# Value products and attention outputs in turn on TensorE, in a windowed-attention and convolution kernel

## The reference

```python
x = x + _L0_conv_ref(_gn(x), W_qkv, W_out, rel_height, rel_width)
x = x + _L1_conv_ref(_gn(x), weight, bias)

# inside _L0_conv_ref: windows of 8x8 queries, 12x12 keys, 4 heads of 32 channels
attn = jnp.einsum('bnd,bmd->bnm', q, k)
attn = attn + rel_pos_emb(q, rel_height, rel_width) + FIXED_MASK
attn = jax.nn.softmax(attn, axis=-1)
out = jnp.einsum('bnm,bmd->bnd', attn, v)
...
return jnp.einsum('bchw,oc->bohw', out, W_out)
```

## Time and profile before

| | |
|---|---|
| time, median of 3 runs | 3672.58 us (3671.35 to 3673.6) |
| profiled execution, its own time | 3670.79 us |
| span of its trace | 3669.0 us |
| PE busy | 3487.6 us (95%) |
| DVE busy | 3365.2 us (92%) |
| ACT busy | 2975.3 us (81%) |
| POOL busy | 2576.8 us (70%) |
| mean granted TensorE clock | 0.991 of full |

### The profile page before, as it was taken

The page is one execution under the profiler, slowest core; times in us unless marked ns, Lnnn a source line. Parts: engine busy times, 40 slices in busy tenths (PEclk is TensorE's granted clock), DMA queues, the critical chain, the costliest instruction groups (busy, mean ns, idle before and its releaser), DMA issues. The chain is left out here.

```text
span 3669.0 us, 127399 instructions
## 1 busy us (share of the span) xinstructions
PE 3487.6 (95%) x51720; PEld 2485.3 (68%) x51720; DVE 3365.2 (92%) x5646; ACT 2975.3 (81%) x5323; POOL 2576.8 (70%) x3345
## 2 busy tenths in 40 slices
PE   0699999999999999899999999999699999999999
PEld 0588888888888878688888888888544444444444
DVE  9799999999999999899999999999799888888887
ACT  0789999999999989799999999999587777777774
POOL 1577777777777777677777777777476666666664
PEclk9999999999999999999999999999899999999999
DMA  9443444344434433233333333333334433443342
GB/s 377 126 128 115 131 132 125 115 131 132 123 116 132 127 83 104 76 90 104 104 98 90 104 104 98 90 104 95 111 144 155 155 146 152 155 153 144 154 155 84
DMA packets 497157, 464.06 MB, mean 126 GB/s; under 512 B 10176, under 2 KB 469824, under 8 KB 478144
## 3 DMA queue, kind: packets, MB, share of 16 engines
q1 hardware_dynamic: 496576, 455.92, 38.9%
HBM read 321.40 MB, written 134.48 MB: 124 GB/s over the span
## 5 line engine op out<-in xcount | busy, mean ns | idle before, releaser
L1001 POOL TENSOR_TENSOR sb_tf<-sb_cf 128x1024 f32<-128x1024 f32 x256 | 609.3, 2381 | 378.6 <-DVE sb_tl L980 370.4
L513 PE MATMUL ps_t<-sb_ident,sb_d 128*108 128x128 f32 x4096 | 664.1, 285 | 5.6 <-ACT sb_pt L706 4.2
L533 PEld LDWEIGHTS ps_s<-sb_kf,sb_qb 128*64 128x64 f32 x16384 | 519.9, 138 | 180.7 <-issue 167.4
L655 DVE TENSOR_TENSOR sb_qb<-ps_q,sb_own_head 128x1024 f32<-128x1024 f32 x512 | 621.2, 1213 | 14.1 <-PE ps_q L495 14.1
L789 POOL TENSOR_TENSOR sb_erel<-sb_brel 128x288 f32<-128x288 f32 x512 | 351.6, 687 | 380.8 <-DVE sb_brel L601 373.0
L897 PE MATMUL ps_c<-sb_th,sb_wc_h 128*128 128x512 f16 x1536 | 584.8, 381 | 20.9 <-DVE sb_tl L980 20.8
L533 PE MATMUL ps_s<-sb_kf,sb_qb 128*64 128x54 f32 x16384 | 586.4, 225 | 11.6 <-DVE sb_scores L635 11.6
L897 PE MATMUL ps_c<-sb_th,sb_wc_l 128*128 128x512 f16 x1536 | 583.7, 380 | 0.0
L897 PE MATMUL ps_c<-sb_tl,sb_wc_h 128*128 128x512 f16 x1536 | 583.6, 380 | 0.0
L819 POOL TENSOR_TENSOR sb_zl<-sb_zf,sb_zh 128x396 f16<-128x396 f32 x512 | 480.9, 939 | 82.5 <-ACT sb_zh L772 82.4
L805 POOL TENSOR_TENSOR sb_prod<-sb_rel,sb_shift 128x192 f32<-128x192 f32 x1024 | 502.7, 512 | 0.0
(11 more groups left out here) (124 smaller groups left out, 8298.0 us busy)
## 6 DMA issues: line engine op xcount, KB each, us to landing
sb_xb<-rows SPq DMA_DIRECT2D x128, 780.0 KB, 7.3
sb_xc<-x SPq DMA_DIRECT2D x64, 1280.0 KB, 5.4
sb_x<-rows SPq DMA_DIRECT2D x128, 512.0 KB, 4.1
x<-sb_x SPq DMA_DIRECT2D x128, 512.0 KB, 3.7
out<-sb_oc SPq DMA_DIRECT2D x64, 1024.0 KB, 3.9
sb_abuf<-rows SPq DMA_DIRECT2D x16, 2048.0 KB, 12.0
sb_st<-rows SPq DMA_DIRECT2D x64, 512.0 KB, 5.1
sb_raw<-wconv SPq DMA_DIRECT2D x1, 576.0 KB, 3.6
```

The source lines that it names most:

```text
L513: last = pe.transpose(ps_t[0:KV, wj * 128:(wj + 1) * 128], d[:, at:at + KV], ident[:])
L533: last = pe.matmul(s_at, qb[:, qc:qc + QB], kf[:, kc:kc + KR], start=True, stop=True)
L655: dve.tensor_tensor(view(qb, 0, 128, vh * QBW + p * NW * QB, [[QB, NW], [QN, HEADS], [1, QN]]), view(ps_q, 0, 128, 0, [[QN, NW], [0, HEADS ...
L1001: pool.tensor_tensor(tf[:, k * TF:(k + 1) * TF], view(cf, 0, 128, c0 + ra * W, [[2 * W, PAIRROWS], [1, W]]), view(cf, 0, 128, c0 + rb * W, ...
```

## The change

The two loops over the parities, first all twelve value products and then all sixteen outputs, become one loop. In it each value product is followed at once by one or two outputs: the first product of a parity by heads 0 and 1, the second by head 2, the third by head 3. The semaphore waits of both stand ahead of the loop, the two signals behind it. The same 28 matmuls are issued with the same operands; no DMA and no instruction of another engine is touched.

```diff
-                            for p in range(PAR):
-                                for c, (z, w) in enumerate(PRODUCTS):
-                                    last = pe.matmul(ps_v[0:KV, p * C:(p + 1) * C],
...
-                            last.then_inc(sem["v_mm"], 1)
...
-                            for p in range(PAR):
-                                py, px = divmod(p, 2)
-                                for hd in range(HEADS):
...
+                        for p in range(PAR):
+                            py, px = divmod(p, 2)
+                            for c, (z, w) in enumerate(PRODUCTS):
+                                if own:
+                                    last_v = pe.matmul(ps_v[0:KV, p * C:(p + 1) * C],
+                                                       z_at(z, vslot, p, GW * WK * vg, [[1, KV]]),
+                                                       w[:, 2 * C:3 * C], start=(c == 0), stop=(c == 2))
+                                for hd in ((0, 1), (2,), (3,))[c] if outputs else ():
...
+                                    last_o = pe.matmul(o_at, v_at, p_at, start=True, stop=True)
+                        if own:
+                            last_v.then_inc(sem["v_mm"], 1)
+                        if outputs:
+                            last_o.then_inc(sem["o_mm"], 1)
```

More of the change, by code:

```diff
@@ L539, in body @@
                             project(n, (g + 1) % PAR, slot + ahead, u + ahead, MOMENTS.get(u) if g == 1 else None)
-                        if on(n - 3, GT):
-                            m = n - 3
+                        own, outputs = on(n - 3, GT), on(n - 4, GT)
+                        if own:
                             vslot, vg = (slot, 0) if g == 3 else (slot - 1, g + 1)
-                            need(pe, sem["vf_done"], m)
-                            for p in range(PAR):
-                                for c, (z, w) in enumerate(PRODUCTS):
-                                    last = pe.matmul(ps_v[0:KV, p * C:(p + 1) * C],
-                                                     z_at(z, vslot, p, GW * WK * vg, [[1, KV]]),
-                                                     w[:, 2 * C:3 * C], start=(c == 0), stop=(c == 2))
-                            last.then_inc(sem["v_mm"], 1)
-                        if on(n - 4, GT):
+                            need(pe, sem["vf_done"], n - 3)
+                        if outputs:
                             m, par = n - 4, g % 2
@@ L563, in body @@
                                                 [[128, GW], [1, QN]])
-                                    last = pe.matmul(o_at, v_at, p_at, start=True, stop=True)
-                            last.then_inc(sem["o_mm"], 1)
+                                    last_o = pe.matmul(o_at, v_at, p_at, start=True, stop=True)
+                        if own:
+                            last_v.then_inc(sem["v_mm"], 1)
+                        if outputs:
+                            last_o.then_inc(sem["o_mm"], 1)
                         if on(n - 3, GT):
```

## The result

The changed kernel takes 6198.8 us (median of 4 runs, 6191.8 to 6201.6) against 3672.1 us for the kernel before: a ratio of 1.688 (95% interval 1.686 to 1.690). The forecast was 6450 us with a range of 5180 to 6980. The drains and the swinging clock both came; the clock's part was smaller than forecast.

What follows compares the result with a forecast made beforehand. TensorE was taken to bound the attention phase. Drains and open weight loads add 3.80 us a turn and the low clock 1.65; 511 turns of 5.45 us on 3671 give 6456 us, forecast as about 6450, range 5180 to 6980.

Steps and rivals of the forecast that it cites:

- TensorE sets the pace, and 511 turns multiply: Attention phase: TensorE binds, so time added to its block counts once in each of 511 turns of 4.83 us.
- The drain, 0.15 us each way: Between value products and outputs: each change of weight width takes about 0.15 us, against 0.055 for a same-width successor.
- The open load of 108 columns, 0.05 us: Before outputs following a value product: their weight load is no longer hidden and adds 0.05 us.
- the second half of a float32 matmul, 0.08: Within each head's outputs: the second record starts 0.08 us after the first, not 0.055.
- The lower bound: Block of value products and outputs: open loads might be hidden, making it 4.3 us and the whole run 5180 us.
- The clock: Thin new block makes the granted clock fall and swing: 1.65 us more a turn, about 6450 us; chance 0.46.
- A fall in the block is undone in the dense rest of the turn, so about 4 us low in every turn: Each attention turn: the clock falls in the block and recovers during dense work, about 4 us low.
- The sign that was named, a mean granted clock near 0.85: Changed profile: a turn of about 10.3 us with mean granted clock near 0.85 would show a swinging clock.
- The clock holds: Rival for the new block: width changes drain but the clock stays full, 5613 us (5180 to 5725); chance 0.38.
- No drain: Rival: alternating neighbours drain cheaply or not at all, but heads no longer share the array, about 4000 us; chance 0.08.
- faster: Rival: outputs run in the shadow of value products and width changes vanish, 3640 us; chance 0.03.
- What is moved for the others: Shifted signals and waits for ACT's copies stay hidden and cost nothing; without that cover 0.3 us a turn, 150 us.

Runs made afterwards that it cites:

- 5180: Not a run: the lower end, in us, of the forecast range of 5180 to 6980 for the changed kernel, which measured 6198.8 us.
- the wide-output pair: Every output matmul takes all 128 value columns as weights, in the changed kernel's alternating order and in the earlier grouped order: 5130.2 and 5119.2 us.
- 7 excursions: Changed kernel with parities 0 and 1 alternating, 2 and 3 grouped: 4674.3 us; for 10, only parity 3 grouped: 5535.7 us.
- the last kernel: Kernel before with its grouped outputs moved directly ahead of the scores, ACT's copy of ps_o behind that of the second transposes: 3656.8 us, ratio 0.9961.

## Why the prediction was right

Step by step, by its own terms:

- **TensorE sets the pace, and 511 turns multiply.** Right. In every kernel here the time follows the turn of TensorE, and the busy time of DVE, ACT and POOL differs from before by no more than 60 us in any of them. The turns are even: from 500 to 900 us their mean is 4.83 us before, as the one turn read.
- **The drain, 0.15 us each way.** Right, also for the way back that the trace of before did not show (0.15 us from the last output to the next product). That it goes with the width and not with data type, tile or waits was argued there from one row; the wide-output pair shows it.
- **The open load of 108 columns, 0.05 us, and the second half of a float32 matmul, 0.08.** 0.04 and 0.08. The block came to 5.03 us for 5.15, and the drains' part to 1880 us for 1942. The lower bound (loads pulled ahead across the change, 4.3 us) is excluded.
- **The clock.** The direction was right and the term mis-sized: 1.65 us a turn forecast, 1.27 measured by the remainder (645 us over 511 turns; forecast 843). The step that missed is "A fall in the block is undone in the dense rest of the turn, so about 4 us low in every turn". The falls come in about six of ten turns, and each lasts 4.8 us, not 4: 3.0 us low in a mean turn of 9.8. The price of low time, 1.7 times, was about right: 1.27 us lost of 3.0 low is a factor of 1.73. Two errors, too many falls and too short ones, partly cancelled. The sign that was named, a mean granted clock near 0.85, also did not follow from the sum, since 4 of 10.3 us low is 0.81; 0.85 was measured. Of the miss of 257 us, 62 lie in the drains and loads and 198 in the clock (the other 3 are rounding and the base).
- **Luck.** That the clock falls at all was preferred by 0.46 to 0.38, mainly on the evidence of one stretch at the end of the attention phase, and the range of 5180 to 6980 held both cases. That the time lies in the range therefore says little about the clock; the traces do.
- **The rivals.** "The clock holds" was the nearest, at 0.38; 5554 us, measured with the dense work spread out, is what it would have been (5613 forecast). The kernels with added work show how near the two cases were: 0.34 us of further matmuls in a turn parts them. "No drain" and "faster" fell with the first timeline.
- **What is moved for the others.** ACT waits 4 us a turn for the values, and TensorE waits for ACT for 1.4 us in the whole run: the cost of nothing was right. One reading was off without effect: the last product stands 0.27 us before the last output, not 0.4 (0.19 to the first record of the outputs and 0.08 to the second).

By the Trainium skill's page TensorE: Matmul & The Clock Gate, section Why this matters for your kernels, idle gaps are what to avoid; here the clock fell in a block without a gap in the records, and the measurement decides.

What stays open is how thin and how long a stretch may be before the clock falls, and what exactly counts as thin. The clock held at 7 excursions and fell in every second turn at 10; it fell with no added columns and held with 64.

## What to carry to other kernels

Matmuls with narrow weights are cheap only in the company of their like: group them, since each step from wide to narrow weights or back cost a drain of 0.09 us here, and a weight load in the open. Four records of 32 columns side by side cost 0.056 us, as much as one value product. When the order of TensorE is changed, read the distances between the starts of matmuls and the granted clock; the busy share said 95% and 97% for two kernels that are 1.69 apart. If the clock swings, try to put dense work into the thin stretch before taking work out. When blocks are moved, follow also what the other engines copy out behind them: in the last kernel only a quarter of the gain arrived, since ACT's copy came too late in half of the turns.

## What the hardware showed that I had not expected

- More work was faster: 12 further matmuls of 64 columns in every turn took the time from 6199 to 5712 us, since they kept the granted clock at 1.00.
- The clock, once low, stayed so into the dense work behind the thin block (from 701.2 to 708.0) and slowed work that had nothing to do with the change: transposes from 0.49 to 0.89 us for four, scores from 1.07 to 1.89.
- The kernel before had a spare change of width in each turn. Its removal gave 0.4%, of 1.7% that the order was worth.
